# Slot numbers on another engine, the zero fill cut into pieces, and a reordered third prologue in a four-layer mixture-of-experts kernel

## The reference

```python
x = x + tanh(g_xattn[0]) * wkv(layernorm(x), ctx)             # a scan over time
x = x + tanh(g_ffn[0])   * moe_top2(layernorm(x), 8 experts of 176, shared of 352)
x = x + tanh(g_xattn[1]) * masked_attention(layernorm(x), ctx, mask)
x = x + tanh(g_ffn[1])   * moe_capacity(layernorm(x), 32 experts of 128, top 4)
x = x + tanh(g_xattn[2]) * attention_qk_norm(layernorm(x), ctx, 32 heads of 8)
x = x + tanh(g_ffn[2])   * moe_zone(layernorm(x), 8 experts of 256, low-rank additions)
x = x + tanh(g_xattn[3]) * attention_int8(layernorm(x), ctx, 16 heads of 16)
x = x + tanh(g_ffn[3])   * moe_top_p(layernorm(x), 8 experts of 512)
```

```python
buf = zeros((E, C, 256)).at[expert, pos].set(x[tok], mode='drop')   # C = 2*N//E = 256 seats
eo  = (silu(buf @ gate) * (buf @ up)) @ down                         # per expert
routed = zeros_like(x).at[tok].add(eo[expert, pos] * weight)
```

## Time and profile before

| what | us |
|---|---|
| median of 3 runs | 1212.91 |
| lowest, highest | 1212.77, 1214.76 |
| profiled execution, own time | 1214.31 |
| its span | 1212.5 |
| PE busy | 924.6 (76%) |
| DVE busy | 651.3 (54%) |
| ACT busy | 521.3 (43%) |
| POOL busy | 389.5 (32%) |

### The profile page before, as it was taken

The page is one execution under the profiler, slowest core; times in us unless marked ns, Lnnn a source line. Parts: engine busy times, 40 slices in busy tenths (PEclk is TensorE's granted clock), DMA queues, the critical chain, the costliest instruction groups (busy, mean ns, idle before and its releaser), DMA issues. The chain is left out here.

```text
span 1212.5 us, 17402 instructions
## 1 busy us (share of the span) xinstructions
PE 924.6 (76%) x6352; PEld 573.0 (47%) x6352; DVE 651.3 (54%) x1360; ACT 521.3 (43%) x885; POOL 389.5 (32%) x367
## 2 busy tenths in 40 slices
PE   6764389986405665656888989887788989999998
PEld 3333245655204444444555545544454555555554
DVE  5965334458834343341444253785576765764443
ACT  3546134432204343442153568435644668543332
POOL 4976023332362333233101134721014533410000
PEclk9875589997657777787965699998998999999999
DMA  4113953430123444433301032541114553443332
GB/s 147 40 52 102 376 149 119 119 99 14 50 109 128 141 121 126 146 111 111 99 1 53 1 104 80 157 131 40 40 28 156 157 157 113 154 140 104 100 97 87
DMA packets 60015, 129.12 MB, mean 106 GB/s; under 512 B 9091, under 2 KB 24849, under 8 KB 59938
## 3 DMA queue, kind: packets, MB, share of 16 engines
q1 hardware_dynamic: 43010, 105.54, 29.0%
q10 hardware_dynamic: 12320, 13.63, 3.2%
q0 software_dynamic: 4608, 8.94, 2.0%
HBM read 83.95 MB, written 48.27 MB: 109 GB/s over the span
## 5 line engine op out<-in xcount | busy, mean ns | idle before, releaser
L1453 PE MATMUL ps<-turned_buf,W 128*128 128x512 f16 x576 | 137.3, 390 | 7.8 <-POOL W L778 5.7
L1453 PE MATMUL ps<-turned_buf,wb 128*128 128x512 f16 x576 | 138.0, 391 | 4.1 <-POOL wb L778 4.0
L2194 DVE SCALAR_TENSOR_TENSOR ctx_sb<-ps,ctx_sb 128x512 f32<-128x512 f32 x96 | 66.3, 691 | 132.7 <-PE ps L1453 83.0
L775 POOL TENSOR_SCALAR W<-W 128x768 f32<-128x768 f32 x32 | 69.3, 2165 | 166.4 <-ACT W L1058 89.4
L1046 ACT ACTIVATE ctxT<-ctx_sb 128x512 f16<-128x512 f32 x96 | 60.3, 628 | 112.9 <-DVE ctx_sb L2194 112.8
L763 POOL DMA_INDIRECT slots<-arena x64 | 63.4, 991 | 130.1 <-ACT arena L1109 107.1
L1522 PE MATMUL ps<-ident,arena 128*128 128x128 f32 x128 | 29.9, 380 | 97.7 <-DMA arena<-seats 97.7
L2201 DVE TENSOR_TENSOR ctxT<-ctx_sb,ctxT 128x512 f16<-128x512 f32 x96 | 68.5, 713 | 65.0 <-ACT ctxT L1046 64.5
L1038 ACT ACTIVATE ctx_sb<-ps 128x512 f32<-128x512 f32 x96 | 57.2, 596 | 91.6 <-PE ps L1453 91.3
L1453 PEld LDWEIGHTS ps<-turned_buf,W 128*128 128x128 f16 x576 | 56.0, 100 | 73.3 <-issue 8.0
L1396 PE MATMUL ps<-turned_buf,W 128*128 128x512 f16 x360 | 87.2, 396 | 2.4 <-issue 2.4
(11 more groups left out here) (396 smaller groups left out, 1855.8 us busy)
## 6 DMA issues: line engine op xcount, KB each, us to landing
W<-in_w SPq DMA_DIRECT2D x79, 384.0 KB, 3.7
seats<-k_norm ACTq DMA_DIRECT2D x1, 9216.0 KB, 26.8
arena<-seats SPq DMA_DIRECT2D x32, 288.0 KB, 3.1
kept<-W SPq DMA_DIRECT2D x24, 384.0 KB, 4.2
kept<-wb SPq DMA_DIRECT2D x24, 384.0 KB, 4.2
W<-kept SPq DMA_DIRECT2D x24, 384.0 KB, 3.0
wb<-kept SPq DMA_DIRECT2D x24, 384.0 KB, 3.1
wb<-in_w SPq DMA_DIRECT2D x16, 384.0 KB, 4.0
```

The lines of the kernel that those rows point to most:

```text
L775: link(nc.gpsimd.tensor_scalar(W[:, n % 2, :], W[:, n % 2, :], WSCALE, None, ALU.mult))
L1453: last = nc.tensor.matmul(bank(4 + n), w4[k % 4][:, w, n * D + c * P:n * D + (c + 1) * P], x16[:, i, c, half * HALF:(half + 1) * HALF], st ...
L2194: nc.vector.scalar_tensor_tensor(h_g[:, g % 2, :], bank(5), 1.0 / WSCALE, h_s[:, g % 2, :], ALU.mult, ALU.mult).then_inc(sem("gated"), 1)
```

## The change

Three edits, independent of each other:

1. `m_dest` gets a buffer per expert. DVE makes the slot numbers at the end of `expert_x(k)`, right after the low halves of the rows of k. POOL keeps only the waits for `e_dest` and `e_y` and the two scatters.
2. The zero fill leaves ACT. SP issues it in 28 pieces, two behind the `wb` loads of each of the 14 tiles of `ffn(0)` (4 or 5 blocks of 128 rows of `seats`, 2 or 3 of `slots`).
3. In the third prologue the products for pairs without a seat of the first six tiles go ahead of `keep_busy`, which has 16 products instead of 32. PE's order is then sums 0 and 1, transposes and queries 0 and 1, sum 2, `turn_q2(0)`, the loop; sum 3 is made at its step n = 1. DVE adds pairs 2 and 3 at steps 0 and 5. The steps of the later pairs' work move a little, and the banks of the sums change.

```diff
-        m_dest = ar.take([3, CT]).bitcast(U32)
+        m_dest = ar.take([E1, CT]).bitcast(U32)
...
-        Q_TURN = (3, 11)
-        Q_PRODUCT = (4, 12)
-        Q_NORM = (1, 8, 19)
-        Q_SCALE = (2, 9, 20)
-        Q_LOW = (3, 5, 10, 13, 21, 23)
+        Q_ADD = (0, 5)
+        X_NORM = (2, 7)
+        Q_TURN = (4, 9)
+        Q_PRODUCT = (6, 11)
+        Q_NORM = (3, 10, 18)
+        Q_SCALE = (4, 11, 19)
+        Q_LOW = (5, 7, 12, 14, 20, 22)
...
+            def clear(i):
+
+                if i == 0:
+                    sp.wait_ge(sem("set_up"), SET_UP["zeros"])
+                no_rows = k_norm[:, 0:2, :, :].rearrange("p k b h -> p (k b h)")
+                for rows, wide in ((seats, ROW), (slots, D)):
+                    j = rows.shape[0] // P
+                    lo, hi = j * i // NT0, j * (i + 1) // NT0
+                    sp.dma_start(rows.rearrange("(j p) d -> p j d", p=P)[:, lo:hi, :],
+                                 no_rows[:, 0:wide].unsqueeze(1).to_broadcast((P, hi - lo, wide))).then_inc(sem("seats_zero"), 16)
...
                         sp.dma_start(wb[lo:hi, i % 2, :], routed[0][row].partition_broadcast(hi - lo))\
                             .then_inc(sem("wb_in", i % 2), 16)
+                    clear(i)
...
-            pool.wait_ge(sem("seats_zero"), 16 * 2)
+            pool.wait_ge(sem("seats_zero"), 16 * 2 * NT0)
...
             for k in range(E1):
-                pool.wait_ge(sem("ex_in", k % 3), 16 * (k // 3 + 1))
-                if k >= 3:
-                    pool.wait_ge(sem("served", k % 3), 16 * CT * (k // 3))
-                nc.gpsimd.tensor_scalar(m_dest[:, k % 3, :], e_x[:, k % 3, :, D + k], -1.0, NOWHERE, ALU.mult, ALU.add)\
-                    .then_inc(sem("e_dest"), 1)
                 pool.wait_ge(sem("e_dest"), k + 1)
                 pool.wait_ge(sem("e_y"), k + 1)
...
-            act.wait_ge(sem("set_up"), SET_UP["zeros"])
-            no_rows = k_norm[:, 0:2, :, :].rearrange("p k b h -> p (k b h)")
-            nc.scalar.dma_start(seats.rearrange("(j p) d -> p j d", p=P),
-                                no_rows[:, 0:ROW].unsqueeze(1).to_broadcast((P, E1 * CAPACITY // P, ROW))).then_inc(sem("seats_zero"), 16)
-            nc.scalar.dma_start(slots.rearrange("(j p) d -> p j d", p=P),
-                                no_rows[:, 0:D].unsqueeze(1).to_broadcast((P, SLOTS // P, D))).then_inc(sem("seats_zero"), 16)
...
-            keep_busy(32, 3)
+            no_seat()
+            keep_busy(16, 3)
             sum_back(0)
             sum_back(1)
             turn_x(0)
             queries(0)
-            sum_back(2)
             turn_x(1)
             queries(1)
-            sum_back(3)
+            sum_back(2)
             turn_q2(0)
             for n in range(8 * B + 2):
                 b = n // 8
+                if n == 1:
+                    sum_back(3)
...
+                nc.vector.tensor_scalar(m_dest[:, k, :], e_x[:, k % 3, :, D + k], -1.0, NOWHERE, ALU.mult, ALU.add)\
+                    .then_inc(sem("e_dest"), 1)
...
-            add_back(2)
             q2_norm(0)
             q2_scale(0)
-            add_back(3)
             q2_lo(0)
```

More of the change, by code:

```diff
@@ L366, in sum_bank @@
         def sum_bank(p):
-            return (4, 6, 0, 1)[p]
+            return (4, 6, 2, 5)[p]
         def x_bank(p):
-            return (5, 7, 5, 7)[p]
+            return (5, 7, 7, 5)[p]
         def q_bank(p):
@@ L762, in _ @@
                 for c in range(CT):
-                    nc.gpsimd.indirect_dma_start(slots, bass.IndirectOffsetOnAxis(ap=m_dest[:, k % 3, c:c + 1], axis=0),
+                    nc.gpsimd.indirect_dma_start(slots, bass.IndirectOffsetOnAxis(ap=m_dest[:, k, c:c + 1], axis=0),
                                                  e_y[k % 3][:, c, :], None, bounds_check=SLOTS - 1, oob_is_err=False)\
@@ L1701, in keep_busy, with no_seat, seatless @@
                                      start=True, stop=True, skip_group_check=True)
-            def sum_back(p):
[L1705 to L1710, removed]
+            def no_seat():
+                pe.wait_ge(sem("back_diag"), 1)
+                pe.wait_ge(sem("wT_half"), 4)
+                pe.wait_ge(sem("e_y"), E1)
+                for i in range(3):
+                    pe.wait_ge(sem("last", i), 16 * len(range(i, E1, 3)))
+                seatless(range(6))
+            def seatless(tiles):
+                for t in tiles:
+                    nc.tensor.matmul(ps[:, sum_bank(t // 2), (t % 2) * D:(t % 2 + 1) * D], over_T[:, t * S:(t + 1) * S], last_rows,
+                                     start=(t % 2 == 0), stop=False, skip_group_check=True)
+            def sum_back(p):
+                if p == 3:
+                    pe.wait_ge(sem("turned"), 2 * KD * 4 + 1)
+                    seatless(range(6, 8))
                 for t in (2 * p, 2 * p + 1):
-                    o = ps[:, sum_bank(p), (t % 2) * D:(t % 2 + 1) * D]
-                    nc.tensor.matmul(o, over_T[:, t * S:(t + 1) * S], last_rows, start=True, stop=False)
                     pe.wait_ge(sem("back", t % 4), 16 * (t // 4 + 1))
                     for i in range(TOP1):
-                        last = nc.tensor.matmul(o, diag(t, i), e_back[:, t % 4, i, :], start=False, stop=(i == TOP1 - 1))
+                        last = nc.tensor.matmul(ps[:, sum_bank(p), (t % 2) * D:(t % 2 + 1) * D], diag(t, i), e_back[:, t % 4, i, :],
+                                                start=False, stop=(i == TOP1 - 1), skip_group_check=True)
                     last.then_inc(sem("back_read"), 1)
             def turn_x(p):
-                if p >= 2:
-                    pe.wait_ge(sem("turned"), 2 * KD * 4 + p - 1)
+                if p == 2:
+                    pe.wait_ge(sem("turned"), 2 * KD * 4 + 2)
                 for t in (2 * p, 2 * p + 1):
@@ L1760, in scores_2 @@
                     pe.wait_ge(sem("q2T"), b + 1)
-                if n < 2:
-                    pe.wait_ge(sem("back_added"), 3 + n)
                 if n >= 2:
@@ L1776, in weigh_v2 @@
                     pe.wait_ge(sem("oT"), n // 4)
+                elif i == 0:
+                    pe.wait_ge(sem("back_added"), 3)
                 for j in range(4):
@@ L2600, in _ @@
             for n in range(8 * B + 2):
-                if n in (0, 6):
-                    normalise_pair(2 + n // 6)
+                if n in Q_ADD:
+                    add_back(2 + Q_ADD.index(n))
+                if n in X_NORM:
+                    normalise_pair(2 + X_NORM.index(n))
                 if n in Q_NORM:
```

## The result

The changed kernel took **1114.35 us** (median of 4 runs, 1108.88 to 1116.33), the kernel before 1213.69 beside it (1212.77 to 1214.76): ratio **0.9174**, 95% interval 0.9140 to 0.9208. Forecast were 1109 us and "faster". The profiled execution took 1114.6 us, with a span of 1112.7, against 1214.3 before.

What follows compares the result with a forecast made beforehand. Bounds: expert row loads waiting for POOL, and ACT blocked by the fill's issue. Gains 77.1 + 1.8 + 19.2 + 6.2 = 104.3 us off 1214.3 give 1110.0, adjusted to 1109 us; range 1088 to 1140.

Steps and rivals of the forecast that it cites:

- POOL's tail: End of the experts: POOL finishes sooner after the last results, 1.8 us gained (0 to 3).
- the change does not reach the rows: Experts, rival: SP's stream stays the tie through last_row, nothing gained there, 1188 us; chance 0.02.
- row loads stay late: Experts, rival: row loads land in near 7 us, 4.4 us per expert, 1132 us; chance 0.16.
- The row load itself: Experts: row load behind SP's last-row issue sets 3.6 us per expert instead of 6.26, 77.1 us gained.
- arithmetic only: Experts, rival: only the arithmetic chain limits, 3.16 us per expert, 12.8 us more gain, 1096 us; chance 0.15.
- the rival of half clock: Experts, rival: PE stays at half clock, 5.65 us per expert, gain there 17.7, 1168 us; chance 0.06.
- The fill, gain: First feed-forward: ACT's first weight split starts 20.27 us earlier, no longer blocked by the fill's issue.
- The fill, charge: First feed-forward: fill pieces ahead of tile 2's weights make them late, 1.0 us charged once (0 to 5).
- The rule weighed there: Fill: skill's rule that issuing elsewhere saves only usually small sequencer time; by it, 19.2 us less gain.
- the fill saves nothing: First feed-forward, rival: the fill's DMA time returns as late tiles, 1128 us; chance 0.03.
- The third prologue: First sum to first scores 11.3 us shorter, part lost to sum 3 in the loop: net 6.2 us (0 to 11.3).
- Slower, if SP's issues block: First feed-forward, rival: 28 fill issues each block SP as the single one did, 1585 us; chance 0.02.

Runs made afterwards that it cites:

- e1: Kernel before the change with only the slot numbers moved from POOL to DVE: 1139.72 us, ratio 0.9395.
- e8: Changed kernel with weight loads halved from expert 4 on, so results differ from the reference's: 1100.88 us, ratio 0.9079.
- e9: Changed kernel with each expert's last-row transfer (1 KB) and its wait moved from SP to POOL, behind the scatters: 1101.84 us, ratio 0.9075.
- e0: Changed kernel run again, unchanged, beside the three parts measured alone: 1113.97 us, ratio 0.9197.
- e6: Changed kernel with SP's load of the last result row one expert further back: 1107.71 us, ratio 0.9120.
- e10: Changed kernel with last rows sent from POOL's queue, but SP still waiting for each expert's result: 1100.21 us, ratio 0.9078.
- e11: Changed kernel with last rows on POOL, fill pieces only from tile 2 on, idle products ahead of products without a seat: 1091.41 us, ratio 0.9007.
- e5: Changed kernel with no fill pieces beside tiles 0 and 1, the fill spread over the other twelve: 1105.47 us, ratio 0.9131.
- e2: Kernel before the change with only the zero fill in 28 pieces from SP: 1199.24 us, ratio 0.9890.
- e3: Kernel before the change with only the new third prologue: 1197.84 us, ratio 0.9869.
- e4: Changed kernel with the idle products ahead of the products without a seat: 1110.89 us, ratio 0.9162.

## Why the prediction was right, point by point

The sum was 104.3 us; the profile shows 99.8, the runs 99.3. What bounds the kernel and what each edit takes away were right. The closeness of the total is in part luck: measured alone, the slot numbers brought 73.1 us for 78.9 (with POOL's tail), the fill 13.6 for 19.2 and the prologue 15.0 for 6.2, and the two shortfalls and the surplus nearly cancel.

- **What bounds the kernel**: right. e1 alone brings 73.1 us, and the large waits for seats went with it (36.5 us in 14 waits, 26.6 of them the start of the stage). With that the rivals "the change does not reach the rows" and "row loads stay late", 4.4 us per expert, are out.
- **Slot numbers by DVE cost nothing**: right. 32 x 0.23 us with no idle time in front of them, and DVE 81 us busy of 121. Where nothing is late an interval is 3.15 us with them (e8, e9), as it is without them in the kernel before.
- **"The row load itself"**, (6.35 + 4.3) / 3 = 3.6 us per expert: 3.65 measured, 75.7 us gained for 77.1 (3.82 and 70.8 in e0). The number held, its reason only in part. The term assumed that every interval is set by the landing of a row load. They change between the chain's 3.15 and 4.1 to 5.6, e6 keeps long ones with no row late, and e10 prices the tie at 3.6 us where the whole loss is 14.8. What the term left out is what SP's small transfer between the loads does: that the size came out is luck. The rival "arithmetic only", 3.16 us, is what e8, e9 and e11 reach.
- **Clock**: right, 0.97 in the stage; the rival of half clock is out.
- **POOL's tail**: 2.0 us for 1.8.
- **The fill, gain**: right; the first split comes 21.4 us sooner, 1.0 of it from ahead of the fill.
- **The fill, charge**: mis-sized. "I charge 1.0 once" measured 5.2 (from 21.4 to 16.2 of lead). I had worked out 2.2 us of lateness for tile 2 by bytes at 373 GB/s and halved it, as part would lie behind PE's running tile. The wait was 4.68 on ACT and 4.15 on PE, not hidden, and PE then ran its next twelve products at half clock, 0.44 us each. e5 gives all of it back. It lay just past the bound that was kept (5 us). With 1.2 us more on the side of the gain, the fill is 3.0 of the 4.5 us that the sum was off by; the experts are another 1.4.
- **The rule weighed there**: without the issue behind the fill, ACT's first split comes 21.4 us sooner. The Trainium skill, "DMA: Bandwidth & Descriptors", section "Issuing engines are not separate DMA queues", calls the sequencer's time usually small relative to the DMA. The trace after disagrees here, as that of before did. e2, which moves the issues from ACT's stream into SP's and cuts them up, gains 13.6 us, and the rival "the fill saves nothing" is out. No run parts the moving from the cutting up.
- **The third prologue**: 6.0 us for 6.2 in this profile, by luck: none of its three terms was right, and the same difference is some 12.4 us in e3's profile and 16.4 in e0's. Between first sum and first scores 13.5 us went, not 11.3 (of the eight products without a seat that were counted there, seven stand between the two in the earlier trace rows's trace, the first being ahead of the first sum). In front of the first sum 3.3 were lost, which the prediction doesn't have: the idle products stand behind the twelve products and, at 0.36 us each (0.23 in e11), run to 482.86, some 3 us longer than the rows of the kernel before took to come (3.9 us from SP's issue, here 475.5). The loop took 2.4 us, not 5.1, and what follows it 1.8 more, but that is this execution: the loop is 149.1 us here and in e9, 142.9 to 146.1 in the eight other profiles of kernels with the three edits, against 146.6 to 146.7 without this edit and 147.4 with it alone. So a cost of sum 3 in the loop isn't shown; what shows is ACT's single wait of 4.30 us for the next scores at 506.51. e3, on its own, gained 15.0 where all of it was thought to be worth 6.2; there the first sum came 4.0 us after SP asked for its rows (567.6 to 571.6), as before the change (3.9), so the 3.3 weren't lost: SP asked 8.7 us after the start of the last result copy (6.6 in the kernel after), and PE was through with products and idle products 12.2 us after it (14.0).
- **Slower, if SP's issues block**: out. The pieces issue in 0.41 to 1.54 us.

## What to carry to other kernels

When a tie between engines is cut, list what else stands in the freed queue: a 1 KB transfer between large loads cost more here than the waiting that it came with. A byte count of a bulk transfer says whether it fits, its place in the queue says who is late; start it behind the first loads that someone waits for. Idle products that keep TensorE's clock up are best put in the place of a wait and right in front of the work that they serve, by these traces: behind twelve products they held the first sum back by 3.3 us. In e4 the move by itself wasn't clearly faster.

## What was not expected of the hardware

- Late releases: ACT stands idle up to 2.4 us (L1102, L1086) while the products that it waits for are done by the trace, only in kernels with the small transfer in SP's queue and whole weight loads close behind it. It is not settled.
- The granted clock of the third attention's loop differs between executions of the same program, and with it the time. Windows over the loop, from first to last scores, kernel after and e0:

```profile
501.20:650.30 149.10, 131.90 (x1167) 77.98 (x1168) 65.47 (x167) 83.11 (x129) 37.30 (x22) 0.74 0.16 49
```

```profile
504.80:647.70 142.90, 125.70 (x1167) 75.04 (x1168) 65.33 (x167) 83.02 (x129) 37.32 (x22) 0.77 0.17 51
```

The loop is 6.2 us longer in the first, at the lower clock, and PE is busy 6.2 us longer for the same products. The whole executions are 5.8 apart (1114.6 and 1108.8), but that isn't the loop alone: at the experts e0 is 4.3 us longer, behind the loop 3.1 shorter. Why the clock differs stays open, and steps of a few us are for that reason better read from several executions.
